# Attention exponentials over two PSUM banks at a time, with four banks for scores and two for maxima

## What is computed

```python
# L0: layer norm with a conditioned bias; L1: bottleneck adapter with generated weights;
# L2: RMS norm, up projection, val * gelu(gate), quantised, down projection, residual
# L3:
xn = ada_rmsnorm(x, t, gamma, beta)
q, k, v = split(xn @ W_q.T), split(xn @ W_k.T), split(xn @ W_v.T)     # 16 heads of 16
attn = softmax(0.25 * einsum('bnqd,bnkd->bnqk', q, k), axis=-1)       # 512 x 512 per head
x = x + a_alpha * (einsum('bnqk,bnkd->bnqd', attn, v) merged @ W_o.T)
x = x + f_alpha * (silu(xn2 @ gate.T) * (xn2 @ hidden.T) @ out_w.T + out_b)
```

## Time and profile before

| | |
|---|---|
| time, median of 3 runs | 754.32 us (751.64 to 755.57) |
| the profiled execution's own time | 750.76 us |
| its span from first to last instruction | 748.8 us |
| PE busy | 639.4 us (85%) |
| DVE busy | 435.7 us (58%) |
| ACT busy | 392.9 us (52%) |
| POOL busy | 55.0 us (7%) |
| mean granted TensorE clock | 0.925 |

### The profile page before, as it was taken

How to read it: one execution, slowest core, us unless ns; L and a number is a source line. 1 busy time by engine, 2 the same in 40 slices (tenths; PEclk the granted TensorE clock), 3 DMA queues, 4 the chain that set the end, 5 groups by cost and what they waited for, 6 DMA issues and landing times.

```text
span 748.8 us, 9919 instructions
## 1 busy us (share of the span) xinstructions
PE 639.4 (85%) x3426; PEld 429.0 (57%) x3426; DVE 435.7 (58%) x866; ACT 392.9 (52%) x748; POOL 55.0 (7%) x91
## 2 busy tenths in 40 slices
PE   2854698799989988799899988799799988899796
PEld 0411477354468767544477777443488776444585
DVE  0541595688165655877164756885465747982344
ACT  1432567156774564267764563367754572468610
POOL 2010210300000003000000003000000011000000
PEclk9856799689989999899999999899989999899899
DMA  8996431421000004220000014220000013220000
GB/s 285 381 383 223 112 112 30 105 44 24 2 0 1 2 29 105 51 44 3 0 1 5 1 29 105 51 45 2 1 1 1 1 20 86 52 43 2 1 1 28
DMA packets 34487, 45.16 MB, mean 60 GB/s; under 512 B 4736, under 2 KB 27392, under 8 KB 34304
## 3 DMA queue, kind: packets, MB, share of 16 engines
q1 hardware_dynamic: 30048, 31.87, 15.0%
q0 software_dynamic: 3872, 11.54, 5.5%
q10 hardware_dynamic: 512, 1.05, 0.4%
HBM read 28.45 MB, written 3.15 MB: 42 GB/s over the span
## 4 chain that ended last, share of the span: by engine, by line
PE 62%; DVE 13%; DMA 12%; ACT 7%; issue 3%; SPq 2%; ACTq 0%; DVEq 0%
PE psum L1180 30%; PE psum L1340 9%; PE psum L1407 7%; PE psum L1396 7%; DVE mx L997 4%; DMA arena<-in_hyp_w 4%; DMA early_pieces<-in_hyp_w 3%; DMA kst<-split 3%; PE psum L1435 2%; DMA qst<-mrow_lo 1%; ACT arena L679 1%; PE psum L1268 1%; PE psum L1302 1%; PE psum L1253 1%; ACT arena L584 1%
## 5 line engine op out<-in xcount | busy, mean ns | idle before, releaser
L679 ACT ACTIVATE arena<-psum 128x512 f32<-128x512 f32 x256 | 141.2, 600 | 82.9 <-PE psum L1396 82.0
L997 DVE TENSOR_REDUCE mx<-psum 128x1 f32<-128x512 f32 x256 | 162.5, 682 | 36.8 <-PE psum L1340 36.3
L1340 PE MATMUL psum<-kst,qst 96*128 96x512 f32 x192 | 85.8, 500 | 17.6 <-DMA kst<-split 12.3
L1180 PE MATMUL psum<-act,ghw_hi 128*128 128x512 f32 (+1 forms) x288 | 97.7, 404 | 2.2 <-ACT act L520 1.2
L1396 PE MATMUL psum<-qst,kst 98*128 98x512 f32 x192 | 82.3, 450 | 4.9 <-DMA qst<-mrow_lo 3.6
L1340 PEld LDWEIGHTS psum<-kst,qst 96*128 96x128 f32 x192 | 41.8, 222 | 55.0 <-DVE mx L997 31.3
L1180 PE MATMUL psum<-upw_hi,kst 128*128 128x512 f32 x256 | 71.4, 400 | 1.8 <-issue 1.3
L1407 PE MATMUL psum<-arena,vals 128*17 128x512 f32 x512 | 67.4, 598 | 1.3 <-ACT arena L679 1.0
L1180 PEld LDWEIGHTS psum<-act,ghw_hi 128*128 128x128 f32 x288 | 58.8, 216 | 14.4 <-DVE act L798 2.2
L1180 PE MATMUL psum<-act,ghw_lo 128*128 128x512 f32 (+1 forms) x144 | 56.9, 396 | 0.0
L432 POOL DMA_DIRECT2D kst<-split x44 | 21.3, 490 | 460.4 <-ACT split L627 389.9
(11 more groups left out here) (183 smaller groups left out, 1060.4 us busy)
## 6 DMA issues: line engine op xcount, KB each, us to landing
early_pieces<-in_hyp_w SPq DMA_DIRECT2D x17, 512.0 KB, 9.3
arena<-in_hyp_w SPq DMA_DIRECT2D x15, 512.0 KB, 9.4
kst<-split POOLq DMA_DIRECT2D x44, 128.0 KB, 4.0
qst<-split SPq DMA_DIRECT2D x72, 64.0 KB, 3.4
arena<-in_up_w POOLq DMA_DIRECT2D x8, 256.0 KB, 5.4
arena<-in_x SPq DMA_DIRECT2D x4, 512.0 KB, 3.9
arena<-in_gh_w POOLq DMA_DIRECT2D x8, 256.0 KB, 3.6
out_x<-arena SPq DMA_DIRECT2D x8, 256.0 KB, 2.3
```

Of the source, the lines that this page charges most:

```text
L679: s.activation(probs[:, kb % 2, i, :], bank[3 + n % RING], ACT.Exp).then_inc(a_p, 1)
L997: v.reduce_max(mx[:, g % 2, col:col + 1], bank[u % RING], AX.X).then_inc(d_max, 1)
L1180: ins = pe.matmul(dst, lhs(a, c), rhs(z, c), start=start and n == 0, stop=stop and n == len(terms) - 1, skip_group_check=skip)
L1340: pe.matmul(bank[u % RING], qst[g % 3][0:KROWS, i, P * t:P * t + P], keys_of(g)[0:KROWS, i // 2, :], start=True, stop=True).then_inc(e_max, 1)
```

## The change

The exponentials of heads i and i + 1 become one instruction over two neighbouring banks, 1024 columns. Scores get four banks, 2 to 5, in two pairs; a score with an even number waits for the exponential two pairs before. Maxima keep the two banks 0 and 1 (`RING` 2), so tile u waits for the reduction of tile u - 2. `a_p` counts pairs. The output transposes and the output projection, which used banks 0, 3, 1 and 2, now use banks 0, 3, 5, 1 and 0. Nothing else moves in any engine's order; the arithmetic is the same.

```diff
-RING = 3
+RING = 2
+PAIR = 2
+SCORE_BANK = 2
+TURNED_BANK = (3, 5)
+ADDED_BANK = (1, 0)
...
-                    cols = HALVES[h] if c == 1 else slice(0, L)
-                    s.activation(oT[:, c, cols], bank[3 * h][:, cols], ACT.Copy).then_inc(a_onT, 1)
+                    cols, src = (HALVES[h], bank[TURNED_BANK[h]]) if c == 1 else (slice(0, L), bank[0])
+                    s.activation(oT[:, c, cols], src[:, cols], ACT.Copy).then_inc(a_onT, 1)
...
-                        s.wait_ge(e_score, b * (NG * T * G) + n + 1)
-                        if i == 0 and g * T + kb >= 2:
-                            s.wait_ge(e_pvk, b * (NG * T) + g * T + kb - 1)
-                        s.activation(probs[:, kb % 2, i, :], bank[3 + n % RING], ACT.Exp).then_inc(a_p, 1)
+                        if i % PAIR == PAIR - 1:
+                            s.wait_ge(e_score, b * (NG * T * G) + n + 1)
+                            if i == PAIR - 1 and g * T + kb >= 2:
+                                s.wait_ge(e_pvk, b * (NG * T) + g * T + kb - 1)
+                            first_bank = SCORE_BANK + n // PAIR % 2 * PAIR
+                            s.activation(probs[:, kb % 2, i - 1:i + 1, :], psum[:, first_bank:first_bank + PAIR, :],
+                                         ACT.Exp).then_inc(a_p, 1)
...
-                    if k >= RING:
-                        pe.wait_ge(a_p, b * (NG * T * G) + k - RING + 1)
+                    if k >= 2 * PAIR and k % PAIR == 0:
+                        pe.wait_ge(a_p, b * (NG * T * G // PAIR) + k // PAIR - 1)
...
-                    pe.matmul(bank[3 + k % RING], keys_of(g)[0:SROWS, i // 2, P * kb:P * kb + P],
+                    pe.matmul(bank[SCORE_BANK + k % (2 * PAIR)], keys_of(g)[0:SROWS, i // 2, P * kb:P * kb + P],
...
-                    pe.wait_ge(a_p, b * (NG * T * G) + (g * T + kb + 1) * G)
+                    pe.wait_ge(a_p, b * (NG * T * G // PAIR) + (g * T + kb + 1) * (G // PAIR))
...
-                        ins = pe.transpose(bank[3 * h][:, P * t:P * t + P], otok[:, t, P * c:P * c + P], ident[:, :])
+                        dst = bank[0] if c == 0 else bank[TURNED_BANK[h]]
+                        ins = pe.transpose(dst[:, P * t:P * t + P], otok[:, t, P * c:P * c + P], ident[:, :])
```

More of the change, by code:

```diff
@@ L1063, in batch @@
                     v.wait_ge(e_wo, b * 2 + h + 1)
-                    v.tensor_tensor(x4_tok[:, pair, :], bank[1 + h].rearrange("p (t d) -> p t d", t=2), x3_tok[:, pair, :], ALU.add
+                    v.tensor_tensor(x4_tok[:, pair, :], bank[ADDED_BANK[h]].rearrange("p (t d) -> p t d", t=2), x3_tok[:, pair, :], ALU.add
                                     ).then_inc(d_x4, 1)
@@ L1434, in attention_out @@
                         pe.wait_ge(d_woalpha, b + 1)
-                    ins = pe.matmul(bank[1 + t // 2][:, D * (t % 2):D * (t % 2) + D], oT[:, c, P * t:P * t + P],
+                    ins = pe.matmul(bank[ADDED_BANK[t // 2]][:, D * (t % 2):D * (t % 2) + D], oT[:, c, P * t:P * t + P],
                                     wo_alpha[:, c, :], start=(c == 0 and t % 2 == 0), stop=(c == C - 1),
```

## The result

The changed kernel takes 803.8 us (801.1 to 805.0) against 753.5 for the kernel before: a ratio of 1.064, 95% interval 1.061 to 1.068, slower. Its profiled execution took 801.06 us with a span of 799.1, 50.3 more than 748.8. In the ratios, runs more than 1.5% above the fastest of the same kernel are left out as slow; this concerns two of the hybrid's six. The direction was as forecast, and so were the two costs in the sum, the pair and the maxima's ring. The size was not: +30.4 us was forecast, and the median lies 0.8 us above the top of the range. A third cost, a low TensorE clock inside the stage, was not in the sum.

The account below looks back on a forecast made before the run. PE's own pace bounds loops with maxima, a PE-ACT-PE round trip those without. Batch 0's 9.1 us and 7.1 us for each of batches 1 to 3 sum to +30.4 us, forecast 784 us, range 765 to 803.

Parts of the forecast that it names:

- The bound and ACT's share: Attention loops: PE's pace or the PE-ACT-PE round trip bounds; saved ACT time is covered by idle time, worth nothing.
- Part 1 and 2, the pair: Exponentials: a pair takes 1.01 us; loops without maxima go from 2.64 to 3.08 us; 2.5 us per batch.
- the +0.3 booked for the head copy: Head copy L657, queued on ACT behind the pair and awaited by the weighing of kb=0: +0.3 us per batch.
- Part 3, two banks in the pure loops: Pure loops with maxima: a maximum waits for the reduction two before; 3.53 against 3.06 us, +0.47 each, four per batch.
- Part 3, the loops with other work: Loops with turn_max, alphas or heads_out: +1.5 us per batch, bounds 0 and 2.5; all eight loops 3.4.
- Part 4, the starts: Start of the stage: batch 0 +2.6 before turn_max and +0.6 behind; batches 1 to 3 +1.2 each, first maxima covered.
- the clock unchanged in the stage: Expected sign in the attention stage: the granted TensorE clock stays as before the change; no cost booked for it.
- Rival 3: PE's gaps lower the granted clock in the stage; +30 us on top, 814 us; sign: clock rows of 0.5; chance 0.08.
- the step from one batch's rows to the cost of the others: Loop costs read from the second batch's rows, applied to every batch: 3.4 plus 2.5 us, batches 1 to 3 7.1 each.
- Rival 1: Two banks of maxima are enough, reductions keep up; 14 us cost, 768 us; chance 0.15.
- rival 2: ACT sets the loops' pace and each pair gives back 0.12 us: 15.4 us faster, 739 us; chance 0.04.
- Rival 4: The exponential runs as two passes, one per bank: 1.13 us a pair, 787 us; chance counted within the forecast's 0.71.

Follow-up runs that it names:

- the hybrid: Kernel before, with pairs in banks 4, 5 and 2, 3 and the weighing behind score 3 only from score 40 of each batch: 748.3 us, ratio 0.985.
- third experiment: Changed kernel with the weighing moved behind score i=3, no longer between the two scores of a pair: 781.9 us, ratio 1.034.
- first experiment: Kernel before with two banks for maxima and nothing else, single exponentials kept: 791.1 us, ratio 1.045.
- fill run: Changed kernel with filler matmuls: 22 before batch 0's first maximum, and 8 and 10 before every batch's first and second score: 799.3 us, ratio 1.057.
- fifth experiment: Changed kernel with the two products of DVE's alphas step moved behind the last maximum: 793.4 us, ratio 1.050.
- second experiment: Changed kernel with single exponentials of 512 columns over four banks, maxima still in two: 790.6 us, ratio 1.044.

## Why the prediction was right in kind and short in size

**The bound and ACT's share: right.** 128 pairs saved ACT 11 us of busy time and the kernel nothing. The sentence of the Trainium skill, Perfetto Trace Analysis, section Optimizing Scalar/DVE Operations, that breaking instructions up can help where ACT isn't saturated but makes bubbles, agrees with the loops behind the maxima: 3.02 us with pairs, 2.60 with singles. The third experiment limits it: with the weighing moved, the pair is as good or better.

**Part 1 and 2, the pair: right, its last 0.3 us by luck.** 1.025 for 1.01; 3.02 for 3.08; +2.5 us per batch for 2.5. In the first experiment, without pairs, the loops behind the maxima are those of the kernel before. But the +0.3 booked for the head copy isn't there: its loop goes from 2.75 to 3.18 us, +0.43 like its neighbours. The first loop behind the maxima, which the count left out, costs 0.32 (2.95 to 3.27 in batch 1), and the two errors cancel.

**Part 3, two banks in the pure loops: right.** 3.53, with each maximum within 0.02 us of its forecast start.

**Part 3, the loops with other work: right where the clock stayed up.** 3.4 per batch was forecast for the eight loops; they cost 4.2 in batch 1 and 6.2 to 6.3 in the others. Batch 3 of the fill run has the clock at 1.00 over all eight:

```profile
693.20:724.10 30.90, 28.97 (x137) 1.00 0.14 27
```

30.90 against 27.85 us is +3.05, a little less than forecast. The two loops around alphas cost +1.2 in batch 1, about what the forecast had for them (0.47 as a pure loop, 0.6 for DVE's absence, and something for turn_max). The low clock is the rest: 1.4 to 1.5 us behind the gap in the other three batches (fifth experiment), and in the first loop, whose weighing is in the low clock: it costs +1.3 to +1.8, and 3.52 us, +0.1 at most over the kernel before, where the filler kept the clock up.

**Part 4, the starts: the largest miss.** 6.8 us forecast, 18.6 measured from the first maximum to the first weighing. In batch 0 the pairs of reductions came 1.57 us apart as forecast (1.54), but PE's order has 18 maxima ahead of turn_max, not 15: +3.3 for 2.6. The four maxima between turn_max and the first score hold that score up too, where the rows' DMA did before: +0.6 for 0. From first score to first weighing it was +1.6 for 0.6, the clock low to the end of it; that the clock is the cause is argued for batch 0, because the filler didn't keep it up there. For batches 1 to 3 I followed the rings by the durations of the kernel before, with its clock coming back at the same point. It came back later: 0.50 over 10.2 us and into the first loop, where it was 0.55 over 7.6 (both rows above). The fill run puts 2.0 to 3.8 us per batch on this.

The first maxima of batches 1 to 3 were forecast at 0 and cost 0.8, 3.3 and 2.4. Rows of other runs tell ring and clock apart. Below are the first maxima with two banks and the clock up (batch 2 of the second experiment), then with three banks and the clock down for a part (batch 1 of the hybrid):

```profile
479.80:496.60 16.80, 15.21 (x79) 1.00 0.26 62
```
```profile
292.90:310.40 17.50, 16.08 (x78) 0.90 0.23 56
```

With the clock up two banks take 16.8 us and three take 15.9, so the ring costs 0.8 to 0.9 us; a stretch of low clock adds some 1.5 us to either, and a longer one in batch 2 of the changed kernel 2.4. The low clock is in 19 of 21 such batches of the seven profiled kernels with two banks and in 6 of 18 of the six with three, though in none of the kernel before as profiled. So a part of the 50.3 us between the two profiles is the luck of that one execution.

**The ledger.** The forecast lacks 19.9 us (50.3 less 30.4). The low clock: 6.7 to 10.8 us at the starts of batches 1 to 3 with their first loops, 4.4 behind alphas, 4.0 in the first maxima of batches 2 and 3, which is 15 to 19 in all. The starts' own ring, too small by 0.7 + 0.6 us in batch 0 and by 0.8 in the first maxima of each later batch, and the later part of batch 0's start at the low clock (1.0, and 1.4 in its first loop), add some 6; smaller terms of the other sign (the rest of the kernel, -1; the way from turn_max to the first score, up to -0.75 in batches 1 and 2; the eight loops) take some of it back. The step that failed is "the clock unchanged in the stage". Rival 3 had named the clock, and its sign, rows of 0.5 inside the stage, came; but it put the cost into the loops without maxima (five in each batch). There the clock stayed at 1.00. It is low elsewhere: the first maxima alone, the start of the scores, the stretch behind the gap at alphas. With that sentence fell the step from one batch's rows to the cost of the others, whose clock differs.

**Rival 1** (two banks are enough) is refuted by the first experiment, **rival 2** (ACT sets the pace) by ACT's idle time and the sign of the result. **Rival 4**, two passes: the row is one of 1.025, not 1.13.

## What to carry to other kernels

Before giving an engine a longer instruction, look at what stands between its two inputs in the producer's order: here one weighing between the two scores of a pair cost 0.4 us a loop, and moving it turned the pair into a gain. A bank taken from a ring is paid where its consumer is away for other work, and the price can be read off as latency plus service time (here 0.54 + 0.68 + 0.05 us) against the time in which the producer comes round the ring. Use the deep ring in the phase that needs it and the other form when the banks are free; and when a change thins out the work of PE in a start-up phase, ask how long the low clock will last, with its own term.

## What was not expected of the hardware

The clock's low level reached into batches differently, though their instructions are the same: 1.00 over batch 1's first maxima and 0.84 over batch 2's, and in other executions it was other batches. Behind the filler of 5.4 us in batch 0 the clock was 0.87 over the row of the first six maxima and 0.50 over the next six. In the fill run a mean clock of 0.926 instead of 0.903 (the run with filler in batch 0 alone) brought no time at the same ratio of 1.057: a higher granted clock is no gain where added work paid for it.
